# One program start reordered: layer norm of tiles 0 and 1 first, the others inside the slots

## What is computed

```python
x = x + _L0_attn_ref(_layernorm(x), q_kernel, kv_kernel, out_kernel, q_norm_scale, k_norm_scale)
x = x + _L0_ffn_ref(_layernorm(x), w_gate, w_up, w_down)
x = x + _L1_attn_ref(_layernorm(x), W_K, W_Q, W_V, W_O)
x = x + _L1_ffn_ref(_layernorm(x), W1, W2, W3)

def _layernorm(x, eps=1e-05):
    return (x - mean(x)) / sqrt(var(x) + eps)

def _L0_attn_ref(x, ...):          # 16 query heads, 8 key/value heads, head size 128
    q, k, v = projections of x
    q = apply_rope(rms_norm(q, q_norm_scale)); k = apply_rope(rms_norm(k, k_norm_scale))
    logits = (q * ATTN_SCALE) @ k, causal, window of 128
    return softmax(logits) @ v @ out_kernel
```

## Time and profile before

| | |
|---|---|
| median of 3 runs | 742.69 us (739.21, 742.69, 742.89) |
| the profiled execution, its own time | 740.21 us |
| its span in the trace | 738.4 us |
| PE busy | 708.9 us, 96% of the span |
| PEld busy | 632.0 us, 86% |
| DVE busy | 502.2 us, 68% |
| ACT busy | 403.6 us, 55% |
| POOL busy | 361.2 us, 49% |
| chain that ended last, by engine | PE 91%, DVE 6%, issue, DMA, POOL and ACT 1% each |

### The profile page before, as it was taken

One profiled execution on the slowest core, in us unless ns is written; L12 is line 12 of the kernel. 1 busy time (PEld: TensorE's weight loads), 2 busy tenths in 40 slices (PEclk: granted clock), 3 DMA queues, 4 the chain that ended last, 5 costly groups with the idle time before them and its releaser, 6 DMA issues.

```text
span 738.4 us, 14876 instructions
## 1 busy us (share of the span) xinstructions
PE 708.9 (96%) x4296; PEld 632.0 (86%) x4296; DVE 502.2 (68%) x1735; ACT 403.6 (55%) x1203; POOL 361.2 (49%) x513
## 2 busy tenths in 40 slices
PE   4899999999999989999899999999999999889998
PEld 3689999999999978888779999999999999877887
DVE  7898888888888878779857454445444444567443
ACT  3476676766667653523246565555555555554221
POOL 4798888888878892002268351413232325317000
PEclk9999999999999989999999999999999999999999
DMA  6010110101020022100011010101011100000000
GB/s 227 1 44 2 44 44 1 43 0 43 0 99 28 0 86 72 44 1 0 16 58 58 1 59 1 59 1 57 17 40 41 58 0 14 3 13 1 1 29 28
DMA packets 9002, 24.64 MB, mean 33 GB/s; under 512 B 896, under 2 KB 3072, under 8 KB 8832
## 3 DMA queue, kind: packets, MB, share of 16 engines
q1 hardware_dynamic: 8240, 22.55, 8.9%
q10 hardware_dynamic: 720, 1.57, 0.6%
HBM read 23.07 MB, written 1.05 MB: 33 GB/s over the span
## 4 chain that ended last, share of the span: by engine, by line
PE 91%; DVE 6%; issue 1%; DMA 1%; POOL 1%; ACT 1%; SPq 0%; DVEq 0%; ACTq 0%
PE bank L309 12%; PE bank L601 12%; PE bank L292 12%; PE bank L286 11%; PE bank L341 8%; PE bank L264 7%; PE bank L321 6%; PE bank L330 6%; PE bank L343 4%; PE bank L263 4%; PE bank L352 3%; PE bank L640 2%; PE bank L644 2%; PE bank L668 1%; DMA x<-in_x 1%
## 5 line engine op out<-in xcount | busy, mean ns | idle before, releaser
L414 ACT ACTIVATE probs<-scores,negmax 128x128 f32<-128x128 f32 (+1 forms) x256 | 115.5, 452 | 43.1 <-DVE negmax L462 42.3
L443 DVE TENSOR_TENSOR enc_lo<-bank,enc_hi 128x256 fp32r<-128x256 f32 x128 | 54.2, 424 | 121.7 <-PE bank L264 111.1
L365 ACT COPY probs_t<-bank 128x384 f32<-128x384 f32 x128 | 61.3, 479 | 126.7 <-PE bank L330 126.7
L506 POOL TENSOR_TENSOR a_hi<-raw_a,zero 128x384 fp32r<-128x384 f32 (+2 forms) x69 | 53.4, 774 | 111.2 <-PE bank L321 107.3
L426 DVE TENSOR_SCALAR probs<-probs,rinv 128x128 f32<-128x128 f32 (+1 forms) x256 | 85.5, 376 | 4.5
L309 PE MATMUL bank<-b_hi,enc_hi 128*128 128x256 f32 x256 | 75.0, 293 | 5.9 <-DVE x L434 5.9
L341 PE MATMUL bank<-probs_t,v 128*128 128x256 f32 x256 | 77.3, 384 | 1.3 <-DVE enc_lo L443 1.2
L264 PE MATMUL bank<-qk 128*128 128x256 f32 x256 | 76.9, 382 | 0.0
L519 POOL TENSOR_TENSOR rms_r<-meansq,neg_half 128x3 f32<-128x3 f32 x64 | 58.2, 909 | 33.2 <-DVE meansq L496 33.1
L212 POOL TENSOR_TENSOR ln_r<-ln_ve,neg_half 128x1 f32<-128x1 f32 x32 | 19.4, 617 | 111.9 <-DVE ln_ve L202 111.9
L309 PE MATMUL bank<-b_hi,enc_lo 128*128 128x256 f32 x256 | 72.6, 284 | 0.0
(11 more groups left out here) (117 smaller groups left out, 2042.6 us busy)
## 6 DMA issues: line engine op xcount, KB each, us to landing
raw_a<-in_wa SPq DMA_DIRECT2D x10, 768.0 KB, 4.4
raw_a<-in_wa SPq DMA_DIRECT2D x9, 512.0 KB, 3.7
raw_b<-in_wb SPq DMA_DIRECT2D x16, 256.0 KB, 2.7
x<-in_x SPq DMA_DIRECT2D x4, 256.0 KB, 5.9
w_a<-in_w2t SPq DMA_DIRECT2D x1, 1024.0 KB, 4.8
raw_a<-in_wax SPq DMA_DIRECT2D x2, 512.0 KB, 3.3
raw_b<-in_wdown SPq DMA_DIRECT2D x2, 512.0 KB, 3.8
raw_a<-in_wa ACTq DMA_DIRECT2D x1, 512.0 KB, 4.6
```

What stands on the lines that cost most here:

```text
L414: nc.scalar.activation(probs[:, c % 4, c0:c1], scores[:, c % 2, c0:c1], ACT.Exp, bias=negmax[:, c % 2, r:r + 1], scale=-1.0, accum_out=row ...
```

## The change

The prologue now carries tiles 0 and 1 alone through the layer norm. Two new functions serve two tiles at once: `ln_dve_stats_two` adds epsilon for two columns, and `ln_pool_two` takes one power of two columns. The statistics of tiles 2 and 3 come behind the low parts of tiles 0 and 1, their `xn` at the prologue's end, and their transposes, high and low parts into `head(-4)`. The statistics of tiles 4 and 5 stand in VectorE's `head(-4)`, those of 6 and 7 in `head(-3)`; transposes of tiles 4 to 7 are in `head` of slots -3 to 0, their high and low parts in slots -2 to 1. GpSimd takes the four powers between and behind the tables, ahead of its first slot. VectorE and GpSimd make only tables 0 and 2; ScalarE copies table 0 to 1 in both. ScalarE's split of the second pair's weights moves from the prologue behind tiles 2 and 3 in `head(-4)`. VectorE waits for the masks in slot -1 and no longer ahead of all slots.

```diff
@@ -205,6 +206,18 @@
             for step in (ln_dve_bn, ln_dve_aggr, ln_dve_ve):
                 for t in tiles:
                     step(dve, st, t)
+
+        def ln_dve_stats_two(dve, st, t):
+            for step in (ln_dve_bn, ln_dve_aggr):
+                for i in (t, t + 1):
+                    step(dve, st, i)
+            dve.wait_ge(ln["mv"], 8 * st + t + 2)
+            nc.vector.tensor_scalar(ln_ve[:, t:t + 2].unsqueeze(2), ln_mv[:, t:t + 2, 1:2], LN_EPS, None,
+                                    ALU.add).then_inc(ln["ve"], 2)
+
+        def ln_pool_two(pool, st, t):
+            pool.wait_ge(ln["ve"], 8 * st + t + 2)
+            nc.gpsimd.tensor_tensor(ln_r[:, t:t + 2], ln_ve[:, t:t + 2], neg_half[:, 0:2], ALU.pow).then_inc(ln["r"], 2)
 
         def ln_pool(pool, st, t):
             i = 8 * st + t
@@ -1081,16 +1094,15 @@
             nc.gpsimd.memset(neg_half[:, :], -0.5).then_inc(s_half, 1)
             pool.wait_ge(s_zero, 1)
             pool.wait_ge(s_half, 1)
-            for t in range(4):
-                ln_pool(pool, 0, t)
+            ln_pool_two(pool, 0, 0)
 
             pool.wait_ge(s_rope, 16)
             pool.wait_ge(s_scq, 1)
-            for a in range(3):
+            for a in (0, 2):
                 nc.gpsimd.tensor_tensor(cos_t[:, :, a, :], cos_c, scl[:, a // 2, :].unsqueeze(1).broadcast_to([P, 2, DH]),
-                                        ALU.mult).then_inc(s_tab, 1)
-            for t in range(4, TILES):
-                ln_pool(pool, 0, t)
+                                        ALU.mult).then_inc(s_cos, 1)
+                ln_pool_two(pool, 0, 2 + a)
+            ln_pool_two(pool, 0, 6)
             slots(pool, 0, pool_slot, lambda c: None, pool_tail(pool, 0))
             for t in range(4):
                 ln_pool(pool, 2, t)
@@ -1109,17 +1121,24 @@
             act.dma_start(cst[:, 768:1536], consts[:, 768:1536]).then_inc(s_mask, 16)
             act.wait_ge(raw_as[0][0], 16)
             nc.scalar.copy(a_w[0][0][:, 0:WA[0]], raw_a[:, 0, 0:WA[0]]).then_inc(at[0]["a0hi"], 1)
-            for t in range(4):
+            for t in range(2):
                 ln_act(act, 0, t, 4 + t)
 
-            act.wait_ge(raw_as[0][1], 16)
-            for part in range(4):
-                cs = slice(part * QA, (part + 1) * QA)
-                nc.scalar.copy(a_w[1][0][:, cs], raw_a[:, 1, cs]).then_inc(at[0]["ahi"], 1)
+            act.wait_ge(s_sin, 1)
+            nc.scalar.copy(sin_t[:, :, 1, :], sin_t[:, :, 0, :]).then_inc(s_second, 1)
+            act.wait_ge(s_cos, 1)
+            nc.scalar.copy(cos_t[:, :, 1, :], cos_t[:, :, 0, :]).then_inc(s_second, 1)
             for L in range(2):
                 def head(c):
-                    if L == 0 and -4 <= c < 0:
-                        ln_act(act, 0, c + 8, 6 + c % 2)
+                    if L == 0 and c == -4:
+                        for t in (2, 3):
+                            ln_act(act, 0, t, 4 + t)
+                        act.wait_ge(raw_as[0][1], 16)
+                        for part in range(4):
+                            cs = slice(part * QA, (part + 1) * QA)
+                            nc.scalar.copy(a_w[1][0][:, cs], raw_a[:, 1, cs]).then_inc(at[0]["ahi"], 1)
+                    elif L == 0 and -2 <= c < 2:
+                        ln_act(act, 0, c + 6, 6 + c % 2)
                     elif L == 1 and c == -2:
                         for t in range(4, 8):
                             ln_act(act, 2, t, LN2_BANK[t])
@@ -1139,31 +1158,30 @@
 
         @block.vector
         def _(dve):
-            for t in (0, 2):
-                dve.wait_ge(s_x[t // 2], 16)
-                ln_dve_stats(dve, 0, t, t + 1)
-            for t in range(4):
-                ln_dve_scale(dve, 0, t)
+            dve.wait_ge(s_x[0], 16)
+            ln_dve_stats_two(dve, 0, 0)
+            ln_dve_scale(dve, 0, 0)
+            ln_dve_scale(dve, 0, 1)
             dve.wait_ge(at[0]["a0hi"], 1)
             nc.vector.tensor_tensor(a_w[0][1][:, 0:WA[0]], raw_a[:, 0, 0:WA[0]], a_w[0][0][:, 0:WA[0]].bitcast(F32),
                                     ALU.subtract).then_inc(at[0]["a0"], 1)
+            ln_dve_lo(dve, 0, 0, 4)
+            ln_dve_lo(dve, 0, 1, 5)
             dve.wait_ge(s_scl, 16)
             nc.vector.tensor_scalar(scl[:, 0::2, :], scl[:, 0::2, :], -ATTN_SCALE, None, ALU.mult).then_inc(s_scq, 1)
-            for t in range(4):
-                ln_dve_lo(dve, 0, t, 4 + t)
+            dve.wait_ge(s_x[1], 16)
+            ln_dve_stats_two(dve, 0, 2)
 
             dve.wait_ge(s_rope, 16)
             dve.wait_ge(s_scq, 1)
-            for a in range(3):
+            for a in (0, 2):
                 nc.vector.tensor_tensor(sin_t[:, :, a, :], sin_c, scl[:, 2 + a // 2, :].unsqueeze(1).broadcast_to([P, 2, DH]),
-                                        ALU.mult).then_inc(s_tab, 1)
-            for t in (4, 6):
-                dve.wait_ge(s_x[t // 2], 16)
-                ln_dve_stats(dve, 0, t, t + 1)
-            ln_dve_scale(dve, 0, 4)
-            ln_dve_scale(dve, 0, 5)
-            dve.wait_ge(s_tab, 6)
-            dve.wait_ge(s_mask, 16)
+                                        ALU.mult).then_inc(s_sin, 1)
+            ln_dve_scale(dve, 0, 2)
+            ln_dve_scale(dve, 0, 3)
+            dve.wait_ge(s_sin, 2)
+            dve.wait_ge(s_cos, 2)
+            dve.wait_ge(s_second, 2)
             for L in range(2):
                 def tail(t):
 
@@ -1181,10 +1199,22 @@
                         ln_dve_ve(dve, st, t)
 
                 def head(c):
-                    if L == 0 and -4 <= c < 0:
-                        if c < -2:
-                            ln_dve_scale(dve, 0, c + 10)
-                        ln_dve_lo(dve, 0, c + 8, 6 + c % 2)
+                    if L == 0 and c == -4:
+                        for t in (2, 3):
+                            ln_dve_lo(dve, 0, t, 4 + t)
+                        dve.wait_ge(s_x[2], 16)
+                        ln_dve_stats_two(dve, 0, 4)
+                    elif L == 0 and c == -3:
+                        ln_dve_scale(dve, 0, 4)
+                        ln_dve_scale(dve, 0, 5)
+                        dve.wait_ge(s_x[3], 16)
+                        ln_dve_stats_two(dve, 0, 6)
+                    elif L == 0 and -2 <= c < 2:
+                        ln_dve_lo(dve, 0, c + 6, 6 + c % 2)
+                        if c < 0:
+                            ln_dve_scale(dve, 0, c + 8)
+                    if L == 0 and c == -1:
+                        dve.wait_ge(s_mask, 16)
                     if L == 0 and -3 <= c < 1:
 
                         cs = slice((c + 3) * QA, (c + 4) * QA)
@@ -1213,13 +1243,16 @@
         @block.tensor
         def _(pe):
             pe.wait_ge(s_ident, 16)
-            for t in range(4):
+            for t in range(2):
                 ln_pe(pe, 0, t, 4 + t)
             for L in range(2):
                 def head(c):
-                    if L == 0 and -4 <= c < 0:
-                        pe.wait_ge(ln["lo"], max(4, c + 7))
-                        ln_pe(pe, 0, c + 8, 6 + c % 2)
+                    if L == 0 and c == -4:
+                        for t in (2, 3):
+                            ln_pe(pe, 0, t, 4 + t)
+                    elif L == 0 and -3 <= c < 1:
+                        pe.wait_ge(ln["lo"], c + 6)
+                        ln_pe(pe, 0, c + 7, 7 + c // 2 * 2 - c)
                     elif L == 1 and c == -3:
                         pe_last_down(pe, 0)
                     elif L == 1 and c == -2:
```

3 lines of the change are left out of this document (2 added, 1 removed).

## The result

The changed kernel took 744.09 us (median of 20 runs, 741.68 to 747.98), the kernel before 740.64 in the same comparison (20 runs, 737.75 to 743.98). The ratio, estimated from all of these runs, is 1.0051 with an interval of 1.0037 to 1.0065 (the quotient of the two medians is 1.0047): slower, by an amount that lies on the prediction's bound of 0.5%. The prediction said 742.9 in a range of 739.4 to 746.4, a shift of +1.5. The time is in the range, the sign is right, and the shift is more than twice the forecast: +3.45 between the medians.

What follows compares the result with a forecast made beforehand. TensorE was taken to bound the kernel from the projection at 34.94 us on; 2.0 later at 22.4 became 0.8 at slot 0's maxima, plus 0.33 twice gave 1.5; 741.4 + 1.5 = 742.9, range 739.4 to 746.4.

Steps and rivals of the forecast that it cites:

- head start of 2.1: Prologue with tiles 0 and 1 alone: projection 0 on TensorE at 8.8 us, 2.1 earlier than 10.94.
- the power of tiles 6 and 7 ahead of tile 0's rotation: On GpSimd, the power waits for VectorE's statistics; rotated tile 0's transposes at 22.4 against 20.44, kernel 2.0 later.
- restart at the half level: TensorE after 6 us idle: projection 3 at 1.2 GHz, from 23.3 to 25.9 us.
- two low parts more in the tight stretch: VectorE, slots 0 and 1: xT_lo of tiles 6 and 7 add 0.33 each; total 1.5, projection 7 at 36.4.
- handing over to TensorE: The chain of waits passes to TensorE for good at about 36.4 us.
- rival 2: Head start survives, tile 0's rotation not held by the power of tiles 6 and 7: 739.3; with its parts, chance 0.15.
- rival 3: TensorE's slow pace lasts through projection 1: 0.7 to 1.0 more in the chain to GpSimd, +2.5, 743.9; chance 0.12.
- the statistics' step: VectorE's statistics of tiles 6 and 7: 0.87, from 18.25 to 19.1, then 0.2 hand-over to GpSimd's power.
- one duration in it can differ: Slot 1's two probs on VectorE: 1.36 beside GpSimd's addition, kept; undisturbed 0.55, and the sum falls to 0.7.
- from the projection at 34.94 us on: Projection of work item 7: from there TensorE alone sets the pace, and a shift is carried to the end.
- Rival 1: Clock stays low after the restart, projections 4, 5 and 6 slow too: 3.4 more, +4.9, 746.3; chance 0.07.
- The copies: ScalarE's two table copies in the prologue: end by 11.5, needed at 11.73, cover 0.2; cost taken as 0.

Runs made afterwards that it cites:

- e1: Changed kernel with GpSimd's power of tiles 6 and 7 moved behind the first item's rotation: 741.76 us, ratio 1.0034 to the kernel before.
- e2: Changed kernel with the power of tiles 4 and 5 behind the first item's rotation, that of 6 and 7 behind the second's: 739.07 us, ratio 0.9998.
- e4: Changed kernel with two more, unread powers of tiles 6 and 7 right ahead of the real one on GpSimd: 744.86 us, ratio 1.0076.
- e7: Changed kernel with epsilon and power taken for each tile apart again, as before the change: 745.22 us, ratio 1.0055.
- e9: Changed kernel with 24 extra matmuls on TensorE in its gap ahead of the first rotated item: 743.96 us, ratio 1.0080.
- e3: Changed kernel with VectorE's four a_lo pieces of the second pair all in slot -3: 745.37 us, ratio 1.0083.
- e10: The changed kernel's same code run once more: 744.77 us, ratio 1.0081 to the kernel before.
- e11: The code of e3 run once more: 742.57 us, ratio 1.0053 to the kernel before.
- e12: e2 with VectorE's statistics of tiles 4 and 5 ahead of the low parts of tiles 2 and 3, ScalarE's a_hi pieces one head later: 739.63 us, ratio 0.9985.
- e5: Changed kernel with the edits of e2 and e3 together: 740.19 us, ratio 1.0008 to the kernel before.

## Why the prediction was right, and by how much it was short

**The mechanism.** It held at each step: the head start of 2.1, the power of tiles 6 and 7 ahead of tile 0's rotation, TensorE idle from 17 to 23, restart at the half level (granted clock 0.50 from 22 to 24), two low parts more in the tight stretch. The handing over to TensorE came later than forecast, at projection 8 (41.40) and not at 36.4. e1, e2 and e4 show it as a cause: out with the powers, and 4.5 us come back; 1.02 more ahead of them, and 1.02 more arrive. My point "GpSimd takes its instructions in the order written" decided against rival 2 rightly; the head start did survive in e2, where the order lets it.

**The sizes.** The forecast of the first rotated transposes was 22.4, measured 23.19. Of the 0.8, 0.5 came through ScalarE, and it is rival 3 that came true: the slow pace lasted until 13.7, through all but the last matmul of projection 1, where 3.5 us from projection 0 on would have been 12.4. Projection 1 ended 0.6 later than forecast, the square of tile 1 began at 16.12, not 15.55, and the xn pair behind it ended 0.5 later. I had priced this at 0.7 to 1.0 and given it 0.12. The other 0.3 is the statistics' step: from its start to GpSimd's power it takes 1.39 (18.76 to 20.15), where the kernel before took 1.09 (13.44 to 14.53) and I had 1.07; 0.2 of it is the two-tile ln_ve, which starts 0.40 behind the aggregates' start instead of 0.2. My 0.87 for what VectorE itself needs was a misreading: 14.31 is where ln_ve starts, and the next statistics start at 14.50, so it is 1.06. That the first sum of squares came at 12.44 for my 12.3 is in part luck: the statistics of tiles 2 and 3 took 1.17 instead of 0.87 and the xn pair 1.06 instead of 0.7, while the two sin tables took 0.76 instead of 1.16.

**The step that failed** is "two low parts more in the tight stretch", with its "one duration in it can differ". I priced each VectorE row between 25 and 37 us at its undisturbed duration and looked for a meeting with GpSimd in one place only, the probs of slot 1. The rows: a_lo ahead of the first scores 1.15 instead of 0.33 (+0.82; the kernel before had 0.41 in this place); the probs of slot 1 1.03 to the scores behind them instead of 1.28 (-0.25); the probs of slot 2 1.29 instead of 0.46 (+0.83). So the scores of slot 0 started at 31.07 and not 29.45: some 0.5 of it is a_lo's meeting, by e7 and e9, and the rest the late restart. Projection 7 came at 37.69 and not 36.4. And "from the projection at 34.94 us on" TensorE sets the pace held for the kernel before only. The low part of tile 7, priced at 0.33, pushed the probs of slot 2 from 0.34 ahead of GpSimd's addition onto it, so that it cost another 0.83, and item 8 was still VectorE's. In sum: +2.43 at the scores of slot 0, +0.32 to projection 7, +0.86 to projection 8 (37.79 and 41.40), and 0.30 given back by projection 10, as TensorE before the change waited at 43.8 us for a rotation: +3.3. That the probs' meeting comes with the moved low part is read from all twelve traces of the new order against the one before; no run took the low part out alone.

In the prediction I had the rule of the Trainium skill (SBUF — State Buffer, "Who interferes with whom") on the table: the later of two conflicting instructions "fully blocks". Here the a_lo that began 0.12 behind GpSimd's addition ended 0.3 behind its end, which is the a_lo's own undisturbed duration, as that rule has it; it has two inputs from SBUF, which the section names as a case of its own. In e7, where a_lo came first, it ran through in 0.41 and the addition took 1.24. I had used the rule for the probs of slot 1 and weighed it for three xn, where it asked for a walk over all pairs.

**Rival 1** (clock low behind the restart) didn't come: projection 4 ran at 0.23 a matmul again, and e9 with e7 shows that even the one slow projection is worth at most 0.7. **The copies** at nothing were right, with 0.29 of cover for my 0.2. **What I didn't foresee** is that a stretch at the half level in the middle of the kernel moves an execution by as much as half the effect (1.7 of 3.3); the range held it, since it was built on the spread of executions.

**The time.** 742.9 was +1.5 on the middle of the runs then known; the shift was +3.3 by the trace and +3.45 by the medians. The bound of 0.5% (3.7 us) lies right there: I gave 0.88 to no change and 0.08 to slower, and the measured 1.0051 is a hair above, with an interval on both sides of it. That 742.9 lies within 1.2 us of 744.09 is helped by the base: I took 741.4 for the kernel before, and its 20 runs gave 740.64. A walk with all port meetings in it would, I think, have put the two chances near even.

What stays open: the medians of nearly all variants lie 0.1 to 2.5 us (e3's 3.9) above what their shift at item 12 gives, against the kernel before in the same comparison. The profiled execution was often among the lowest (e3, e10, e11, e12). The mean granted clocks say a part of the rest. The stretch at the restart costs the changed kernel's mean 0.005, so an execution without a stretch in the middle should read 0.995; all 26 on record read 0.993 or less. The kernel before, whose restart costs 0.002, reads 0.997 or more, which leaves no room for one in the middle, in 29 of the 66 executions run beside e1 to e12. e2, whose start is at the full clock, reads 0.998 or less in all of its 11, so it has one too, although it is earlier than the kernel before: this is where its 1.2 us may go. Not so in e5, 5 of whose 12 executions leave no room for one. So in the changed kernel stretches in the middle are more frequent, and e2 has them without being late; what makes them so stays open.

## What to carry to other kernels

On an engine that takes its instructions in order, a small instruction with a late input is a barrier: before moving one forward, list everything behind it and ask whose input is ready sooner. Where VectorE and GpSimd are both nearly unbroken, walk the two timelines against each other row by row, since one meeting cost up to 0.83 us beside an addition of 1.0, and price it in every slot until the chain leaves VectorE. A small piece put ahead of another instruction can push that one into a meeting, and then costs more than its own length (0.33 became 1.16 here). A piece of work that fills idle time in one order is in the way in another (e3 and e5), so fill gaps last.

## What the runs showed of the hardware that I had not expected

- A 128x256 a_lo on VectorE took 0.33 alone and 1.15 beside GpSimd's 128x384 addition; two 128x128 probs took 0.55 alone and 1.11 to 1.39 beside it, in every kernel; two 128x256 xn took 0.72 to 0.73 in most places, but 1.14 beside the cos table on GpSimd, in the changed kernel at 11.38 and in e2 and e12. An a_lo that began 0.05 ahead of the addition (e7) took 0.41.
- The two-tile ln_ve, which waits for the aggregate right ahead of it on its own engine, started 0.40 behind the first aggregate in every two-tile place; the single-tile ones, the first of which waits for an aggregate one instruction further ahead, 0.21 (e7 and the kernel before).
- GpSimd's power took 0.54 for one column (half of the 1.08 for a pair), 0.70 to 0.78 for two and mostly 0.84 to 0.87 for three.
- A gap of 2.83 us in TensorE's work was followed by the half level (e5, 1.2 GHz, 0.43 a matmul for projection 4), one of 1.44 in e2 was not, but one of 1.37 in the kernel before was (0.56 and 0.50 from 18 us on), so the length of the last gap alone didn't decide it; and the same code had a stretch at 0.50 from 362 to 364 us in one execution and at 1.00 in the next.
